# Row-maximum scores of four heads in one batch of matmuls, and new orders of work on all engines, in the attention layer of a four-layer graph network

## The reference

```python
qkv = h @ W                                    # h: (16, 512, 128), W: (128, 384)
q, k, v = qkv[0], qkv[1], qkv[2]               # each (batch, 4 heads, 512, 32)
mask = jnp.where(adj == 0, -jnp.inf, 0.0)      # (512, 512), the same for all
scores = jnp.einsum('bhid,bhjd->bhij', q, k) / np.sqrt(HEAD_DIM) + mask
attn = jax.nn.softmax(scores, axis=-1)
out = jnp.einsum('bhij,bhjd->bhid', attn, v)
# then: x = _layernorm(x + out, axis=-1)
```

## Time and profile before

| | |
|---|---|
| median of 3 runs | 969.47 us |
| the runs | 965.02 to 971.21 us |
| span of the profiled execution | 965.1 us |
| PE busy | 905.8 us (94%) |
| DVE busy | 641.5 us (66%) |
| ACT busy | 508.7 us (53%) |
| POOL busy | 382.7 us (40%) |

### The profile page before, as it was taken

One profiled execution on the slowest core, in us unless ns is written; L12 is line 12 of the kernel. 1 busy time (PEld: TensorE's weight loads), 2 busy tenths in 40 slices (PEclk: granted clock), 3 DMA queues, 4 the chain that ended last, 5 costly groups with the idle time before them and its releaser, 6 DMA issues. The chain is left out here.

```text
span 965.1 us, 20989 instructions
## 1 busy us (share of the span) xinstructions
PE 905.8 (94%) x6054; PEld 646.9 (67%) x6054; DVE 641.5 (66%) x1944; ACT 508.7 (53%) x919; POOL 382.7 (40%) x433
## 2 busy tenths in 40 slices
PE   6999999999999699977789999999999998999996
PEld 5799999999999688833345544555445453677775
DVE  4754554554554576646466777777777764899997
ACT  4323121121121245555356777777777767788884
POOL 4011121021020130000246777878778777355554
PEclk9999999999999899979889999999999999999999
DMA  8000000000000100000033334333333342011111
GB/s 245 23 12 12 12 23 12 12 22 11 11 11 0 30 15 0 0 1 0 1 79 77 78 71 87 72 79 85 66 81 83 66 87 46 1 33 33 33 33 44
DMA packets 34236, 40.68 MB, mean 42 GB/s; under 512 B 6672, under 2 KB 17552, under 8 KB 34192
## 3 DMA queue, kind: packets, MB, share of 16 engines
q1 hardware_dynamic: 32816, 39.87, 17.3%
q10 hardware_dynamic: 1376, 0.27, 0.1%
HBM read 6.43 MB, written 4.19 MB: 11 GB/s over the span
## 5 line engine op out<-in xcount | busy, mean ns | idle before, releaser
L1754 DVE CUSTOM_DVE_ANT_0 junk<-bank,mask_ij 128x512 bf16<-128x512 f32 x256 | 166.6, 688 | 78.2 <-PE bank L1844 75.6
L1617 POOL TENSOR_TENSOR half_sum<-prob 128x1024 f32<-128x1024 f32 x64 | 151.9, 2381 | 13.6 <-ACT prob L1691 13.6
L1691 ACT ACTIVATE prob<-wide 128x1024 f32<-128x1024 f32 x128 | 125.2, 1017 | 37.2 <-PE wide L1861 32.7
L431 ACT CAST yT<-wide 128x512 fp32r<-128x512 f32 x48 | 28.2, 589 | 206.1 <-PE wide L827 156.8
L531 POOL TENSOR_TENSOR Xr<-Xf,Xr 128x512 fp32r<-128x512 f32 x16 | 20.4, 1292 | 168.1 <-ACT Xr L426 167.9
L1844 PE MATMUL bank<-qkT 32*128 32x512 f32 x256 | 77.1, 504 | 5.2 <-DVE mx L1754 4.3
L1857 PE MATMUL wide<-qk_st 128*128 128x512 f32 x256 | 76.4, 421 | 0.9 <-issue 0.6
L1439 PEld LDWEIGHTS bank<-Wh,pr 128*128 128x128 f32 x512 | 65.3, 191 | 13.5 <-ACT pr L1292 5.3
L59 PE MATMUL bank<-z,L3T_hi 128*128 128x256 f32 x256 | 74.2, 290 | 0.0
L60 PE MATMUL bank<-z,L3T_hi 128*128 128x256 f32 x256 | 73.7, 288 | 0.0
L61 PE MATMUL bank<-z,L3T_lo 128*128 128x256 f32 x256 | 73.7, 288 | 0.0
(11 more groups left out here) (301 smaller groups left out, 2296.1 us busy)
## 6 DMA issues: line engine op xcount, KB each, us to landing
qk_st<-qkT SPq DMA_DIRECT2D x192, 128.0 KB, 2.4
out_dram<-rc SPq DMA_DIRECT2D x15, 256.0 KB, 2.3
Xf<-X SPq DMA_DIRECT2D x14, 256.0 KB, 2.3
A<-in_adj_dram SPq DMA_DIRECT2D x4, 256.0 KB, 4.9
qk_st<-neg_row SPq DMA_DIRECT2D x64, 2.0 KB
Xf<-in_x_dram SPq DMA_DIRECT2D x2, 256.0 KB, 7.0
mask_q<-mask_ji SPq DMA_DIRECT2D x16, 32.0 KB, 1.8
w<-in_L_gnn_W_dram SPq DMA_DIRECT2D x2, 128.0 KB, 2.4
```

The source lines that it names most:

```text
L1617: pool.tensor_tensor(flat(half_sum[h][:]), flat(prob[bp][h][:, 0:2]), flat(prob[bp][h][:, 2:4]), ALU.add).then_inc(h_sum, 1)
L1691: act.activation(flat(prob[bp][h][:, 2 * half:2 * half + 2]), wide[half][:], ACT.Exp, scale=SCALE).then_inc(t_exp, 1)
L1754: dve.tensor_tensor_reduce(out=junk[hh][:], in0=bank[4 + hh][:], in1=m.mask_ij[:, i], scale=1.0, scalar=3.0 * MASKED, op0=ALU.add, op1=ALU ...
```

## The change

Layer 2 alone is changed. The eight items s0 to s7 of two heads become four, s0 to s3, of all four heads for one row tile; their four outputs go to `ROWS`, banks 0, 1, 4 and 5. Banks 0 and 1 are those of the precise scores' first half, so an s now also waits for the exponential E(2h) of the t before it, and a t waits for the first two maxima of the s before it (`before` finds which); t now fills banks 2 and 3 first. m and mr go, and n and nr take all 16 columns at once. r moves from POOL to DVE. The banks of the ring are given by name, x is released by xh in place of xc, and xl waits for xh. All five orders are new, with items up to seven steps back where there were five; the loops run to step 18 and the tails are rewritten (PE's new tail runs "v.15 t2.14 D0.13 D1.13 n.15 t3.14 3x.0 d.13 o.13 t0.15 3j.0 V0.14 V1.14 t1.15 ..."). The diff, cut to its core:

```diff
-        PE_ORDER = staged("t0:3 s0:2 m:3 D0:4 D1:4 V0:4 V1:4 s1:2 t1:3 s2:2 V2:4 V3:4 s3:2 x:1 t2:3 s4:2 n:2 d:4 o:4 "
-                          "s5:2 T:0 q:1 t3:3 s6:2 k:1 v:2 s7:2")
-        ACT_ORDER = staged("kh:2 E0:3 mr:3 N:0 E1:3 Y:1 e:4 E2:3 E3:3 y:5 f:4 xh:1 xc:1 nr:2 E4:3 E5:3 qh:1 E6:3 E7:3 vc:2")
-        DVE_ORDER = staged("u5:2 R:0 ql:1 u6:2 u7:2 kl:1 B:0 u0:1 b:4 u1:1 u2:1 u3:1 u4:1 c1:3 c2:3")
-        POOL_ORDER = staged("xl:1 r:4 S2:3 X:1 S3:3 g1:0 g2:4 S0:2 S1:2")
-        SP_ORDER = staged("st3:1 dn1:0 st0:0 dn0:0 st1:0 dn3:0 dn2:0 st2:0")
...
-        RING = [(name, back) for name, back in PE_ORDER if name in ("T", "x", "q", "k", "v", "n", "m", "D0", "V0", "d", "o")]
-        ring = {name: bank[6 + n % 2] for n, (name, _) in enumerate(RING)}
+        PE_ORDER = staged("v:4 k:3 t2:5 D0:6 D1:6 s0:3 x:2 n:4 t3:5 d:6 T:0 s1:3 o:6 t0:4 V0:5 V1:5 s2:3 q:2 t1:4 V2:5 V3:5 s3:3")
+        ACT_ORDER = staged("E0:5 E1:5 Y:2 qh:3 E2:5 E3:5 f:6 vc:4 kh:3 N:0 E4:5 E5:5 e:6 xc:2 nr:4 E6:5 E7:5 y:7 xh:2")
+        DVE_ORDER = staged("ql:3 b:7 u3:4 kl:3 u0:3 R:0 c1:6 u1:3 B:0 c2:6 u2:3 r:6")
+        POOL_ORDER = staged("X:2 g2:7 S0:5 S1:5 xl:2 S2:5 S3:5 g1:0")
+        SP_ORDER = staged("dn2:1 st3:1 st0:0 st1:0 dn3:1 dn0:0 st2:0 dn1:0")
+
+        ring = {name: bank[6 + k] for name, k in staged("T:1 x:1 k:0 v:1 q:1 n:0 D0:1 V0:0 d:0 o:1")}
+        RING = [item for item in PE_ORDER if item[0] in ring]
+        ROWS = [bank[0], bank[1], bank[4], bank[5]]
+        SHARED = 2
...
         def released(name, b):
 
-            return {"x": (x_c, after(b, 1)), "q": (q_lo, after(b, 1)), "k": (k_lo, after(b, 1)),
-                    "v": (v_c, after(b, 1)), "n": (n_row[0], after(b, 1)), "m": (n_row[1], after(b, 1)),
-                    "D0": (d_c, after(b, 1)), "V0": (o_c, after(b, 1)), "d": (rcp, after(b, 1)),
-                    "o": (o_n, after(b, 1)), "T": (res1, after(b, 1))}[name]
+            return {"x": (x_hi, after(b, 1)), "q": (q_lo, after(b, 1)), "k": (k_lo, after(b, 1)),
+                    "v": (v_c, after(b, 1)), "n": (n_row, after(b, 1)), "D0": (d_c, after(b, 1)),
+                    "V0": (o_c, after(b, 1)), "d": (rcp, after(b, 1)), "o": (o_n, after(b, 1)),
+                    "T": (res1, after(b, 1))}[name]
+
+        def before(name, b, kind):
+
+            names = [n for n, _ in PE_ORDER]
+            at = names.index(name)
+            k = max(range(len(names)), key=lambda k: (names[k][0] == kind, (k - at - 1) % len(names)))
+            return int(names[k][1]), b + dict(PE_ORDER)[name] - PE_ORDER[k][1] - (k > at)
...
-                    pool.wait_ge(x_c, after(b, 1))
+                    pool.wait_ge(x_hi, after(b, 1))
...
-                elif name == "r":
-                    pool.wait_ge(o_n, after(b, 1))
-                    pool.wait_ge(x_f, after(b, 1))
-                    hold(pool, gate)
-                    pool.tensor_tensor(flat(r[:]), flat(r[:]), batch_flat(m.X, b), ALU.add).then_inc(o_r, 1)
-
-            run(pool, POOL_ORDER, work, last=16)
...
-                elif name in ("nr", "mr"):
-                    p = "nm".index(name[0])
-                    act.wait_ge(n_ps[p], after(b, 1))
-                    for h in (2 * p, 2 * p + 1):
+                elif name == "nr":
+                    act.wait_ge(n_ps, after(b, 1))
...
-            run(act, ACT_ORDER, work, last=17)
+            run(act, ACT_ORDER, work, last=18)
...
-                    k = int(name[1])
-                    pair, i = divmod(k, NT)
-                    for hh in range(2):
-                        tile = 2 * k + hh
-                        col = (2 * pair + hh) * NT + i
+                    i = int(name[1])
+                    for h in range(H):
+                        tile = i * H + h
...
-                        dve.tensor_tensor_reduce(out=junk[hh][:], in0=bank[4 + hh][:], in1=m.mask_ij[:, i],
+                        dve.tensor_tensor_reduce(out=junk[h % 2][:], in0=ROWS[h][:], in1=m.mask_ij[:, i],
                                                  scale=1.0, scalar=3.0 * MASKED, op0=ALU.add, op1=ALU.max,
                                                  accum_out=mx[bp][:, col:col + 1]).then_inc(s_mx, 1)
...
+                elif name == "r":
+                    dve.wait_ge(o_n, after(b, 1))
+                    dve.wait_ge(x_f, after(b, 1))
+                    hold(dve, gate)
+                    dve.tensor_tensor(flat(r[:]), flat(r[:]), batch_flat(m.X, b), ALU.add).then_inc(o_r, 1)
...
-            run(dve, DVE_ORDER, work, last=16)
...
-            SPARE = {("T", 0): 14, ("x", 1): 3, ("k", 1): 2, ("s0", 2): 5, ("s1", 2): 3, ("s2", 2): 3, ("s3", 2): 2, ("s4", 2): 2}
+            SPARE = {("T", 0): 12, ("T", 1): 5, ("x", 2): 3, ("q", 2): 3, ("k", 3): 2, ("s0", 3): 4, ("s1", 3): 3, ("s2", 3): 3}
 
             def work(name, b, bp, s, alive):
                 product(name, b, bp, s, alive)
-                for _ in range(SPARE.get((name, s), 0) if isinstance(s, int) and s < 3 else 0):
-                    pe.matmul(bank[0][:], m.identb[:], m.mask_ji[:, 0], start=True, stop=True)
+                for _ in range(SPARE.get((name, s), 0) if isinstance(s, int) and s < 4 else 0):
+                    pe.matmul(bank[2][:], m.identb[:], m.mask_ji[:, 0], start=True, stop=True)
...
-                    k = int(name[1])
-                    pair, i = divmod(k, NT)
-                    if k == 0:
+                    i = int(name[1])
+                    if i == 0:
                         pe.wait_ge(q_hi, after(b, 1))
                         pe.wait_ge(k_hi, after(b, 1))
-                    for hh in range(2):
-                        pe.wait_ge(s_mx, after(b, TILES, 2 * k + hh - 1))
-                        c = slice((2 * pair + hh) * HD, (2 * pair + hh + 1) * HD)
-                        pe.matmul(bank[4 + hh][:], qkT[bp][c, Q_HI, i * P:i * P + P], qkT[bp][c, K_HI],
+                    pe.wait_ge(s_mx, after(b, TILES, i * H))
+                    h, bt = before(name, b, "t")
+                    if not isinstance(bt, int) or bt >= 0:
+                        pe.wait_ge(t_exp, after(bt, EXPS, 2 * h + 1))
+                    for h in range(H):
+                        c = slice(h * HD, h * HD + HD)
+                        pe.matmul(ROWS[h][:], qkT[bp][c, Q_HI, i * P:i * P + P], qkT[bp][c, K_HI],
                                   start=True, stop=True).then_inc(s_ps, 1)
...
-                elif name in ("n", "m"):
-                    p = "nm".index(name)
-                    pe.wait_ge(s_mx, after(b, TILES, (p + 1) * TILES // 2))
-                    pe.transpose(out[0:2 * NT, 0:P], mx[bp][:, 2 * NT * p:2 * NT * (p + 1)], m.ident[:]).then_inc(n_ps[p], 1)
+                elif name == "n":
+                    pe.wait_ge(s_mx, after(b, TILES))
+                    pe.transpose(out[0:TILES, 0:P], mx[bp][:], m.ident[:]).then_inc(n_ps, 1)
                 elif name[0] == "t":
                     k = int(name[1])
                     pe.wait_ge(row_in[k], after(b, 16))
                     pe.wait_ge(stacked[k], after(b, STACKED))
-                    for j in range(NT):
-                        if j % 2 == 0:
-                            pe.wait_ge(t_exp, after(b, EXPS, 2 * k - 1 + j // 2))
+                    pe.wait_ge(t_exp, after(b, EXPS, 2 * k))
+                    i, bs = before(name, b, "s")
+                    if isinstance(bs, int) and bs >= B:
+                        i, bs = NT - 1, B - 1
+                    for j in (2, 3, 0, 1):
+                        if j < SHARED:
+                            pe.wait_ge(s_mx, after(bs, TILES, i * H + j + 1))
                         pe.matmul(bank[j][:], k_st[:, k, j * P:j * P + P], q_st[:, k], start=True, stop=True)
                     for c in range(4):
                         for j in range(NT):
...
-            run(pe, PE_ORDER, work, last=17)
+            run(pe, PE_ORDER, work, last=18)
```

More of the change, by code:

```diff
@@ L1486, in layers2_3 @@
         mx = [sb(f"mx{k}", [P, TILES]) for k in range(2)]
-        neg_row = [sb(f"neg_row{k}", [2 * NT, P], F32R) for k in range(2)]
+        neg_row = sb("neg_row", [TILES, P], F32R)
         late = [sb(f"prob{h}", [P, NT, N]) for h in (2, 3)]
@@ L1508, in layers2_3 @@
         s_ps = sem("scores"); s_mx = sem("row_max")
-        n_ps = [sem(f"max_turned{p}") for p in range(2)]
-        n_row = [sem(f"neg_row_out{p}") for p in range(2)]
+        n_ps = sem("max_turned"); n_row = sem("neg_row_out")
         row_in = [sem(f"row_in{h}") for h in range(H)]
@@ L1562, in tail @@
                     s = b + backs[name]
-                    second(name, b, b % 2, s, [0 <= s - k < B for k in range(6)])
+                    second(name, b, b % 2, s, [0 <= s - k < B for k in range(8)])
         @block.sync
@@ L1593, in _ @@
         def _(pool):
-            for s in (x_f, x_lo, o_r):
+            for s in (x_f, x_lo):
                 pool.sem_inc(s, CREDIT)
@@ L1618, in work @@
                                        ALU.add).then_inc(h_sum, 1)
```

(45 more changed lines are left out.)

13 lines of the change are left out of this document (7 added, 6 removed).

## The result

The changed kernel takes 1009.16 us (median of 4 runs, 1007.55 to 1013.95), the kernel before 969.59 (4 runs). The ratio is 1.043, with a 95% interval of 1.039 to 1.046: 40 us slower.

A forecast was written before the change was run, and what follows sets the result against it. PE's queue bound the old kernel's step; the new one would be bound by T's wait for xh. 29 + 4 + 22 = 55 us on 965.1 gave 1020, plus 4.4 for the median 1025, range 990 to 1060.

The forecast's parts named there:

- The walk from E to E: Layer 2's chain from exponential to exponential (E0, E2, E4, E6) through shared banks: a step of 23.6 us against 20.44.
- E0 to E2: From the exponential E0 on ACT to E2, with V0 and V1 ahead of s2 on PE: 4.82 us.
- E2 to E4: From the exponential E2 on ACT to E4, with s3, v and k ahead of t2 on PE: 5.51 us.
- E4 to E6: From the exponential E4 on ACT to E6, with D0 and D1 ahead of s0 on PE: 4.73 us.
- E6 to E0: From E6 to the next E0, T waiting for xh: 8.52 us; without the wait 4.77, the step 19.8.
- The quad: Four matmuls of s on PE cost what a pair costs, 0.43 us: 1.7 us less PE work a step.
- The first rival: Only PE's own queue counts, 18.7 us plus 3.8 idle: step 22.5 us, 990 us at most; chance 0.10.
- The clock: Half clock behind each whole wait, where t0, V0 and V1 run: 2.0 us on 11 steps, 22 us.
- The sum: 29 us from the intervals t0(0) to t0(15), 4 ahead of t0(0), 22 for the clock: 55 us more.
- r on DVE: r's 0.68 us between u2 and u3 costs nothing in a step, with 0.4 us of slack left.
- The rival: r on DVE and POOL's half sums exclude each other: r loses 2.0 us on some 13 steps, 1051 us; chance 0.10.
- The rival on the other side: T's wait is hidden if xh runs within some 2 us of t3: step 19.8 us, 961 us, or 945; chance 0.06.

The follow-up runs named there:

- Experiments 1 and 2: Against the changed kernel: xh moved right behind xc on ACT, 957.88 us; or T in the ring's first bank with c1 ahead of R on DVE, 985.75 us.
- experiment 6: The kernel with xh behind xc, the four matmuls of each s taken apart into two and two: 978.97 us, ratio 1.009 to the kernel before.
- experiment 3: The changed kernel with 12 useless matmuls behind d filling PE's idle time ahead of T: 1000.48 us, ratio 1.035 to the kernel before.
- experiment 7: The kernel with xh behind xc, r on DVE moved ahead of u2 into POOL's half sums: 969.56 us, ratio 1.001 to the kernel before.
- experiment 5: The changed kernel with r back on POOL behind g1: 1019.85 us; the same in the kernel with xh behind xc: 960.58 us.

## Why the prediction came out right, step by step

**The direction and the mechanism** are as told. T starts 0.13 us behind xh's end (631.53 + 0.57 = 632.10, T at 632.23), after 3.59 us of idle where 3.8 were worked out. Experiments 1 and 2 show that it is this wait and this bank: with xh early it is gone, with T in the other bank it is o's.

**The walk from E to E** against one step after (from the rows of ACT above) and one with xh early (from the E4 at 620.26 us to the next, at 639.65):

| | predicted | after | predicted without the wait | xh early |
|---|---|---|---|---|
| E0 to E2 | 4.82 | 4.59 | 4.82 | 5.14 |
| E2 to E4 | 5.51 | 5.37 | 5.51 | 4.91 |
| E4 to E6 | 4.73 | 4.82 | 4.73 | 4.95 |
| E6 to E0 | 8.52 | 8.97 | 4.77 | 4.39 |
| step | 23.6 | 23.75 | 19.8 | 19.39 |

Every interval worked out from the earlier trace rows held to about half a microsecond, those of the shared banks too, which the kernel before never shows. In the last column E2 is late behind qh, which waits for a DMA of SP there, and so the next is shorter; the walk had cost SP's queue at nothing. From step to step it is 4.8 to 5.5 there.

**The quad** costs what a pair costs, as put (experiment 6). PE's work fell by a little more than was said, from 20.38 us a step to 18.39 with xh early (608.27 to 627.56 us, at full clock), where 18.7 was put; the kernel could not use it while T waited.

**The first rival**, PE's own queue alone, does not hold: with the clock filled a step is 23.05 us and not 22.5, with xh early it is 19.3 and not the 18.7 of PE's work alone, and 2.4 us of PE's queue added in experiment 6 made the step only 1 us longer. Its sum was also off: 22.5 against 20.44 over 15 steps is 31 us, not 20, so it gives some 1000 us, and the 990 that the range took for its low end does not follow from it.

**The clock is the term that was mis-sized.** The prediction took 2.0 us for each of 11 waits, 22 us; the fill of experiment 3 gives back 7 to 9, some 0.85 a step. The fall itself came as read from the earlier trace rows, but earlier than put, and largely where PE waits anyway: in the step above the clock is at 0.59 from 633.5 to 637.0, while o waits for R and t0's shared matmuls for the maxima, and it is back before V0. The 0.85 that it still costs are on the chain, in t0's last matmuls. The price at its upper end, V0 and V1 doubled, is real as well: it was paid in step 6 (24.88 us where the walk had 22.0), there with V0 and V1 at half clock:
```profile
516.15 3.64 PE L1890 MATMUL bank<-prob,v 128*32 128x512 f32 x16
```

**The sum** then was 29 + 4 + 22 = 55; measured are 40.5 on the profiled executions. In its terms: the intervals from t0(0) to t0(15) without the clock were put at 335.7 us and came out at 345.1 with it, 9.4 more; ahead of t0(0) 2.5 in place of 4; behind t0(15) -0.8 in place of 0. With the fill of experiment 3 the intervals are 336.5, so the clock costs 8.6 us or a little more, since the fill does not reach every fall. That this meets 335.7 is in part luck, since two misses cancel: steps 7 to 15 take 207.5 there where 212.4 were put, all the others 129.0 where 123.3 were put. The steps 16 and 17, in which o waits for xh, took 44.4 us where 43 were put.

**r on DVE** cost nothing in the steady steps, as put. The rival was right on the mechanism, though: r and a half sum do exclude each other (experiment 7), with 1.5 us for an r of 0.69. In the changed kernel it was met once, behind the full steps. What kept it out was close to what the prediction named: in the changed kernel POOL is idle while r runs in every full step (at 618.09 us, for one), and with xh early it is in short instructions. The Trainium skill (SBUF — State Buffer, section "SBUF: two separate sides") has this lock for a DVE instruction with two SBUF inputs against a GpSimd one that reads SBUF; the traces of experiment 7 agree, with 0.54 to 0.56 us of r behind the end of the half sum 15 times. The POOL instruction on 128 x 4 elements shown there reads SBUF too and did not hold r; there the trace and the rule differ.

**The rival on the other side** did not have its condition met. Its time was nearly right: with xh out of the way the kernel takes 954 to 958 us, where 961 were put for a step of 19.8.

What stays open: the bank sharing's own share in the 19.3 us, since no version without it was run (all eight banks are in use), and why the half clock lasts near 7 us in some steps and 3.5 in others.

## What to carry to other kernels

When a shared buffer is given out by turns, follow each item to the last reader of the item before it, in that reader's own queue: one copy that stands behind two exponentials and a norm kept PE idle for 3.6 us a step, and moving it by four places was worth 5% of the kernel. Price a chain across engines by its hand-overs, from start to start, on the kernel before: that walk foretold steps of an unseen order within 3% (23.6 us for 23.05 with the clock filled, 19.8 for 19.3); with its price for the clock it was 7% high (25.6 for 24.03). A stall's second price, the clock, depends on what runs behind the stall, so bound it from both sides and take the upper end only where full work follows at once.

## What the hardware showed beyond what was expected

- The half clock behind a wait of the same 3.6 us was over after some 3.5 us in the changed kernel's steps 8 to 15 (0.59 over 633.5 to 637.0 us, then 1.00), and lasted near 7 us in some steps of the kernel of experiment 5 (0.52 over 635.0 to 641.5 us, with PE busy for 6.23 of the 6.5), so that steps with the same work differ by 2 us.
- An addition on DVE with both operands in SBUF, 0.69 us alone, took 2.70 us beside a half sum of 2.4 us on POOL, and a POOL instruction of 0.19 us beside it 0.52. Whenever it met the end of a half sum in experiment 7, it ended 0.54 to 0.56 us behind that end.
- Four matmuls on 32 rows each, into four banks, start within 0.01 us of each other and take 0.50 us together.
